# A down projection planned as three stages on PE, and the order of all queues fitted anew

## What is computed

```python
x = x + 0.5 * ffn(layernorm(x), w_gate, w_up, w_down)
x = x + attn(layernorm(x), Wq, Wk, Wv, Wproj, lq1, lk1, lq2, lk2)
x = x + 0.5 * ffn(layernorm(x), w_gate, w_up, w_down)
```

```python
gate = fp4(x) @ fp4(w_gate).T
y    = fp4(x) @ fp4(w_up).T
out  = fp4(silu(gate) * y) @ fp4(w_down).T
```

## Time and profile before

| | |
|---|---|
| time, median of 3 runs | 2385.82 us (2385.47 to 2386.98) |
| the profiled execution | 2386.57 us, span 2384.8 us |
| PE busy | 2036.0 us, 85% of the span |
| DVE busy | 1832.7 us, 77% |
| ACT busy | 1643.2 us, 69% |
| POOL busy | 1372.6 us, 58% |
| mean granted clock of PE | 0.954 of full speed |

### The profile page before, as it was taken

One profiled execution on the slowest core, in us unless ns is written; L12 is line 12 of the kernel. 1 busy time (PEld: TensorE's weight loads), 2 busy tenths in 40 slices (PEclk: granted clock), 3 DMA queues, 4 the chain that ended last, 5 costly groups with the idle time before them and its releaser, 6 DMA issues. The chain is left out here.

```text
span 2384.8 us, 39387 instructions
## 1 busy us (share of the span) xinstructions
PE 2036.0 (85%) x13502; PEld 832.5 (35%) x13502; DVE 1832.7 (77%) x3871; ACT 1643.2 (69%) x2468; POOL 1372.6 (58%) x1328
## 2 busy tenths in 40 slices
PE   2578898989998988899989989899989988988865
PEld 1233333333324333333334333333333433332222
DVE  6898997778847999968847998977856998844334
ACT  2235677777686867777777767677877776678852
POOL 3667666555736666755735676755744675642313
PEclk9689999999999999999999999999999999999987
DMA  3223332220412322231412332231311242230101
GB/s 81 45 40 65 58 61 56 50 60 15 76 34 50 56 64 56 40 76 27 77 39 34 54 74 48 50 59 46 69 43 34 45 69 52 53 59 10 34 1 42
DMA packets 409907, 119.37 MB, mean 50 GB/s; under 512 B 390638, under 2 KB 409454, under 8 KB 409710
## 3 DMA queue, kind: packets, MB, share of 16 engines
q1 hardware_dynamic: 409710, 116.86, 25.6%
HBM read 11.96 MB, written 8.39 MB: 9 GB/s over the span
## 5 line engine op out<-in xcount | busy, mean ns | idle before, releaser
L1085 ACT ACTIVATE probs<-psum_s 128x1024 f32<-128x1024 f32 (+3 forms) x1280 | 1073.6, 898 | 181.8 <-PE psum_s L1376 137.0
L1394 PE MATMUL psum_o<-probs,v_sb 128*32 128x512 f32 (+3 forms) x5120 | 594.3, 553 | 35.9 <-POOL probs L1008 24.7
L1340 PE MATMUL shared<-w_gu_T,xT 128*128 128x480 f16 (+1 forms) x2304 | 507.1, 371 | 101.2 <-DMA xT<-x 46.3
L1376 PE MATMUL psum_s<-q_stack,k_stack 64*128 64x512 f16 (+3 forms) x2560 | 394.2, 358 | 103.6 <-ACT probs L1085 97.3
L1340 PEld LDWEIGHTS shared<-w_gu_T,xT 128*128 128x128 f16 x2304 | 215.2, 99 | 390.9 <-issue 111.9
L1353 PE MATMUL shared<-w_down_T,hT 128*128 128x256 f16 (+1 forms) x2176 | 301.0, 283 | 35.4 <-DVE hq L1175 16.1
L1022 ACT ACTIVATE hq<-shared,tanh_scale 128x240 f32<-128x240 f32 (+1 forms) x384 | 173.1, 456 | 189.3 <-PE shared L1340 181.8
L1008 POOL TENSOR_SCALAR_AFFINE_SELECT probs<-probs 128x512 f32<-128x512 f32 x256 | 189.1, 746 | 182.0 <-ACT probs L1085 181.4
L952 POOL TENSOR_TENSOR hq<-hq,rscale 128x704 f32<-128x704 f32 x128 | 195.5, 1528 | 143.7 <-DVE rscale L1119 140.6
L1376 PEld LDWEIGHTS psum_s<-q_stack,k_stack 64*128 64x128 f16 x2560 | 93.9, 94 | 500.2 <-ACT probs L1085 395.9
L983 POOL TENSOR_TENSOR h<-hq,h 128x704 f16<-128x704 f32 x128 | 204.7, 1599 | 96.7 <-ACT h L1038 96.7
(11 more groups left out here) (120 smaller groups left out, 2492.2 us busy)
## 6 DMA issues: line engine op xcount, KB each, us to landing
xb<-L_attn_x SPq DMA_DIRECT2D x16, 512.0 KB, 4.0
out<-xb SPq DMA_DIRECT2D x16, 512.0 KB, 2.9
hT<-h SPq DMA_TRANSPOSE x128, 3.5
xT<-x SPq DMA_TRANSPOSE x64, 3.1
k_stack<-st_k SPq DMA_TRANSPOSE x64, 3.3
q_stack<-st_q SPq DMA_TRANSPOSE x64, 3.3
k_stack<-L_ffn_w_down SPq DMA_DIRECT2D x1, 704.0 KB, 9.0
k_stack<-L_ffn_w_gate SPq DMA_DIRECT2D x1, 480.0 KB, 5.3
```

Source lines behind the costliest of these rows:

```text
L1085: nc.scalar.activation(probs[:, s % 3, 2 * u:2 * u + 2, q0:CHUNK], psum_s[u][:, :, q0:CHUNK], ACT.Exp, scale=HD ** -0.5 / QK_SCALE ** 2).t ...
L1340: last = nc.tensor.matmul(bank(e)[:, 0:2 * (hi - lo)], xs[:, x, t % 2, k, :], w_gu_T[:, w, k, 2 * lo:2 * hi], start=n == 0, stop=n == len( ...
L1376: last = nc.tensor.matmul(psum_s[u][:, j, q0:CHUNK], k_stack[half, at, h, kt % NTC * P:(kt % NTC + 1) * P], q_stack[half, c % 2, h, q0:CHU ...
L1394: last = nc.tensor.matmul(psum_o[at:at + VD, q0:CHUNK], v_sb[:, kt // NTC % SLOTS * NTC + kt % NTC, 2 * g + u, :], probs[:, s % 3, 2 * u + ...
```

## The change

A tile's `down` becomes three stages, `down_1`, `down_2` and `down`, with six, six and five of the 17 matmuls. They are chained by their needs, so they run in this order and into the same bank, but the planner may put other stages of PE between them. The first takes the bank, waits for it and for the landed transpose; the last frees the `hT16` buffer and increments the semaphore that `add_down` waits for. Beside that all the numbers of `DUE` and nearly all of `COST` are new, and the costs given for `scores` and `values` are slightly higher, so the order of every queue is another.

```diff
-DUE = dict(lead=149, spans=(364, 841, 126, 1498), tail=190257702039, early=-0.24, mlp1=(5, 23), qkv=(-128, 101), qk=(-106, 112), out=(-290, 61), mlp2=(169, 118),
...
+DUE = dict(lead=756, spans=(50, 445, 21, 79111), tail=9217700384204, early=0.13, mlp1=(66, 6), qkv=(-118, 79), qk=(-124, 106), out=(-523, 100), mlp2=(461, 64),
...
+PIECES = ("down_1", "down_2", "down")
...
-            divide_h=1.46, divide_x=1.1, down=2.07, gate=0.82, grid_h=1.1, grid_x=0.8, head_stats=3.3,
...
-            low_x=1.35, mask=0.68, norm_heads=0.45, norm_qk=0.88, norm_x=0.82, points_h=1.1, points_x=0.8,
...
+            divide_h=1.53, divide_x=1.22, down=0.63, down_1=0.77, down_2=0.77, gate=0.82, grid_h=1.14,
...
+            low_h=1.6, low_qk=2.57, low_x=1.29, mask=0.75, norm_heads=0.46, norm_qk=0.91, norm_x=0.84,
+            points_h=1.33, points_x=1.07, project_out=0.92, project_qk=1.84, project_v=0.92, quant_h=1.65,
...
                 dn = ("down", pas, t)
-                fill(dn, 2.1, dt + 13, [("turn_h", "h", *key)], [], [("hT16", key)])
+                add(("down_1", *key), "tensor", .7, dt + 13, [("turn_h", "h", *key)], [("bank", dn)])
+                add(("down_2", *key), "tensor", .7, dt + 13.01, [("down_1", *key)])
+                add(dn, "tensor", .7, dt + 13.02, [("down_2", *key)], [], [("hT16", key)])
...
-                        if e in BANK and BANK[e][1]:
-                            pe.wait_ge(bank_free[BANK[e][0]], BANK[e][1])
+                        first = ("down", *e[1:]) if e[0] == PIECES[0] else e
+                        if first in BANK and BANK[first][1] and e[0] not in PIECES[1:]:
+                            pe.wait_ge(bank_free[BANK[first][0]], BANK[first][1])
...
-                        elif e[0] == "down":
+                        elif e[0] in PIECES:
                             pas, t = e[1:]
-                            pe.wait_ge(*landed("h", (pas, t)))
+                            dn = ("down", pas, t)
+                            if e[0] == PIECES[0]:
+                                pe.wait_ge(*landed("h", (pas, t)))
...
-                            for i, (k, n, w) in enumerate(parts):
-                                last = nc.tensor.matmul(bank(e)[:, 0:C], hs[0:n, k, :], w_down_T[0:n, w, :],
+                            piece = -(-len(parts) // len(PIECES))
+                            mine = range(len(parts))[piece * PIECES.index(e[0]):][:piece]
+                            for i in mine:
+                                k, n, w = parts[i]
+                                last = nc.tensor.matmul(bank(dn)[:, 0:C], hs[0:n, k, :], w_down_T[0:n, w, :],
                                                         start=i == 0, stop=i == len(parts) - 1)
-                            last.then_inc(full(e)[0], 1)
+                            if e == dn:
+                                last.then_inc(full(dn)[0], 1)
```

More of the change, by code:

```diff
@@ L51 @@
 SLOTS = NCH + 1
-DUE = dict(lead=149, spans=(364, 841, 126, 1498), tail=190257702039, early=-0.24, mlp1=(5, 23), qkv=(-128, 101), qk=(-106, 112), out=(-290, 61), mlp2=(169, 118),
[L57 to L64, removed]
+DUE = dict(lead=756, spans=(50, 445, 21, 79111), tail=9217700384204, early=0.13, mlp1=(66, 6), qkv=(-118, 79), qk=(-124, 106), out=(-523, 100), mlp2=(461, 64),
+           nudge=dict(add_down=27, add_out=-44, copy_o=-6, copy_xT=9, dequant_h=-9, divide_x=9,
+                      down=-44, down_1=37, down_2=15, exp=5, grid_h=-32, grid_x=29, head_stats=-15,
+                      heads_out=73, hidden=49, high_h=-104, high_qk=-45, high_x=1, load=15, low_h=2,
+                      low_qk=9, low_x=48, mask=-10, norm_qk=4, norm_x=-11, points_h=-52,
+                      points_x=-15, project_out=30, project_v=-38, quant_x=42, read_qk=11,
+                      read_v=43, rms=33, rope=-6, rope_add=2, rstd=57, scores=-78, square_h=3,
+                      square_x=23, stats=-114, store=20, tanh=-9, transpose_o=30, transpose_x=62,
+                      turn_h=-54, turn_qk=-43, turn_x=18, values=23))
 ST = 2
@@ L78 @@
 HALF = P // 2
+PIECES = ("down_1", "down_2", "down")
 KTILES = [(lo + i * (hi - lo) // 2, (hi - lo) // 2) for lo, hi in PARTS for i in range(2)]
[L81 to L87 removed]
+COST = dict(add_down=0.46, add_out=0.42, copy_o=0.68, copy_xT=0.39, dequant_h=1.46, dequant_x=1.14,
+            divide_h=1.53, divide_x=1.22, down=0.63, down_1=0.77, down_2=0.77, gate=0.82, grid_h=1.14,
+            grid_x=0.93, head_stats=2.75, heads_out=3.03, hidden=1.29, high_h=0.79, high_qk=1.16, high_x=0.63,
+            low_h=1.6, low_qk=2.57, low_x=1.29, mask=0.75, norm_heads=0.46, norm_qk=0.91, norm_x=0.84,
+            points_h=1.33, points_x=1.07, project_out=0.92, project_qk=1.84, project_v=0.92, quant_h=1.65,
+            quant_x=2.84, read_qk=0.6, read_v=0.38, rms=4.05, rope=1.93, rope_add=1.38, rstd=2.71,
+            square_h=0.79, square_x=0.63, stats=1.82, tanh=0.46, transpose_o=0.59, transpose_x=0.3)
 OVERLAP = dict(tensor=0.0, vector=0.08, scalar=0.1, gpsimd=0.04, sync=0.0)
@@ L350, in whole_plan @@
                 before = s - 1 + u, 1 - u
-                add(("scores", s, u), "tensor", .22 * w, d + u * .1,
+                add(("scores", s, u), "tensor", .23 * w, d + u * .1,
                     [("turn_qk", tiles[-1]), ("scores", s - 1, 1) if s else None],
@@ L358, in whole_plan @@
             d += (CHUNK - q0) * k
-            add(("values", s), "tensor", .87 * w, d, [("mask", s) if diag is not None else ("exp", s, 1),
+            add(("values", s), "tensor", .90 * w, d, [("mask", s) if diag is not None else ("exp", s, 1),
                                                       ("values", s - 1) if s else None, ("read_v", tiles[-1])],
```

## The result

The changed kernel is slower: 2394.44 us median (2389.56 to 2396.93, 6 runs) beside 2385.76 us for the kernel before, a ratio of 1.0033 with a 95% interval of 1.0021 to 1.0045. A second set of runs gave 1.0026 (1.0016 to 1.0037). I had forecast 0.8% faster; the time lies inside the range, on its other side.

What follows compares the result with a forecast made beforehand. PE, 85% busy, was taken as bound partly by its work and partly by its holes, 139.5 us of them before attention. -25 + 10 - 5 = -20 us gave 2366 us, 0.8% faster, with a range of 2342 to 2396.

Steps and rivals of the forecast that it cites:

- The split, -25 us: PE's holes before attention: a piece is a third of the down, so what waits behind it waits less, 25 us gained.
- 0.265 x 139.5 = 37 us: Share of PE's 139.5 us of holes before attention ascribed to downs, by their 26.5% of shared-bank time.
- The price, +10 us: Changes of form on PE when attention stands inside a down: one joint in every second down, 58 x 0.18 us.
- The refit, -5 us: All queues reordered with costs nearer the trace: 5 us gained of 65.5 us of holes before shared-bank work, bounds +-26 us.
- The start: Up to 206 us, before the first `scores`: set by DVE, so no change was expected.
- the end: The 83.7 us behind the last `values`: no attention left to stand between pieces, so no change was expected.
- what is held longer: An opened down keeps a shared bank and an hT buffer about 1.6 us per joint longer; put at nothing in the sum.
- the mechanism in the time line: PE in a `down` and three `hidden` starts a ready `scores` late, so its exps come late and `values` waits 1.29 us.
- slower by the change of forms: Rival on PE: the planner opens many joints without the gain, price 21 us (2407 us) or 42 us (2428 us); chance 0.22.
- the range's slow end: Upper limit of the forecast time, 2396 us: the +10 us price of changes of form with no gain.

Runs made afterwards that it cites:

- e15: Changed kernel with the planner adding the 0.11 us for a change of form after choosing a stage, not before; ratio 1.0818 of the kernel before.
- e3: Kernel before, its order kept, downs in three pieces with at most one attention stage let into each joint; ratio 0.9999 of the kernel before.
- e14: Kernel before, attention let in between any two stages of shared-bank work where its inputs are planned ready, downs whole; ratio 1.0239.
- e13: Kernel before, attention let in between any two stages of shared-bank work and into the joints of downs in pieces; ratio 1.0272.
- e2: Kernel before, its order kept, downs in three pieces with up to three attention stages let into each joint; ratio 1.0060 of the kernel before.
- e6: Changed kernel with at most one attention stage let into each joint that its plan left closed; ratio 1.0075 of the kernel before.
- e1: Changed kernel, its order kept, with the three pieces of every down put together again; ratio 1.0068 of the kernel before.
- e4: Kernel before with the new costs alone, under its old due times and with no pieces; ratio 1.0210 of the kernel before.
- e7: Changed kernel's new costs and new due times with the down as one whole stage; ratio 1.0236 of the kernel before.
- e8: Kernel before with one due number changed by one (pace of the qk stages, 112 to 113); ratio 1.0050 of the kernel before.

## Why the prediction was wrong, point by point

**The split, -25 us: the step that failed, twice.** I wrote that PE's blocks hold attention back and that a piece holds it back a third as long. First, the planner can't put attention there. The choice rule, which the section on the kernel before quotes, adds 0.11 us to the start of a stage of another form before it compares. The next piece can start at once, so it wins against every `scores` and `values` whatever their due times are; only a stage of the same form can win. Nine joints are the result, where I had counted on 58, and e15 shows the rule at work. I should have followed the rule through for one down; the rival that the change doesn't do what it says would have had most of the chance. Second, the gain isn't there when attention is let in by hand: 0 of 25 us in e3, holes up by 19 in e14.

The term came from 0.265 x 139.5 = 37 us, a share by PE's time for each kind of work, and the trace of the kernel before already spoke against it. Of the 139.5 us only 6.0 have a down among the four stages of PE ahead of the hole. Within 4 us of the end of a down lie 41 us of holes, 30%, and such stretches are 34% of the time of attention, so the holes don't gather behind downs. In the time line of the earlier trace rows too, the down is the small part. The next `scores` needed the first of the two exps that the row merges, and that one ends at 1512.36. Of the 4.7 us until 1517.07, 1.0 lie in the down and 3.7 in the three `hidden`, which the change leaves whole. The releaser, an exp, was in the row. How much of the holes is ACT's own time and how much lateness that other blocks cause is not separated by any run.

**The price, +10 us: not incurred, since no attention stage stands in a joint.** Changes of form fell by 20. Where they were added between stages they cost about 0.1 us each (e13, e14), near the 0.09 of the time line; where a joint of a down took them, 0.02 to 0.05 (e2, e3, e6).

**The refit, -5 us: wrong in sign, within its bounds.** The new order is the whole of the +8: with the nine joints closed it is +16 (e1), so they, within this fit, work the other way. The argument was that costs nearer to the trace give a better order. e4 shows that they need not: new costs give a new order, and in it the costs are others again. That due times, costs and stage list were fitted together is the reading that e4, e7 and e8 share; it is not shown apart from them. The new fit is as good a fit as the old to 0.3%, and e8 moves the time by more than that with one step of one number. Which of the new numbers brings the 10.7 us before attention is not settled; each part taken out of the fit (e1, e4, e7) changed the whole by more than the effect.

**What held.** The start (204.4 us for the first `scores`) and the end (82.9 us behind the last `values`, 83.7 before) stayed; what is held longer cost nothing that shows; each engine's count of instructions is the same, and the total is 10 lower; the mechanism in the time line, PE late by exps, is real. The rival "slower by the change of forms" had the right sign and another mechanism. That the time fell inside my range is luck: it is the range's slow end, which stood for a price that wasn't paid.

## What to carry to other kernels

When a change gives a planner a new freedom, follow its choice rule by hand for one case before pricing the freedom: a stage that can start at once beats one that must change form first, however early it is due. A hole isn't charged by shares of busy time to the work that PE did before it: look where the holes stand, and what released them. Ask the planner, too: its own length for the old order under the new costs gave 3 us. And the numbers that steer an ordering belong to one exact set of stages and costs: new costs alone made this kernel 2% slower, and a single step of one number moved it by 0.5%, so a difference of 0.3% between two fits says nothing about the idea that came with the second.

## What the runs showed of the hardware that I had not expected

A change of form on PE costs 0.096 us when it stands between whole stages (e14: 49.8 us of busy time for 521; 0.11 within attention), but 0.02 to 0.05 us where stages of attention stand between the pieces of a down (within attention, e2: 4.3 us for 153; e3: 10.8 for 198; e6: 4 to 7 for 179). These are single profiles, and two of the same kernel differ by 2.8 us there. The Trainium skill (TensorEngine Tiling, section Key Properties) says that a change of tiling mode drains the engine; e14's 0.096 us agrees with a small loss at each change, the runs with opened downs with a smaller one, and no run shows the drain itself. Letting `scores` go ahead of other work moved PE's idle time without making or saving any: 348.8 us before, 348.4 in e14. The same instruction on the same data takes other times in another order: `points_x` has a mean of 1.072 us before and 0.981 after, 8% less, with the kernel slower, and `points_h` 1.327 us before, 1.285 after and 1.217 in e4.
